# Attention of a four-layer kernel: products for the maxima sent one by one, the second set's maxima turned a stage earlier, the output matrix split in pieces

## The chip, the cores and the metric

The kernel runs on one core of a Trainium2 chip. The metric is the device time of one execution in microseconds; the median of three runs counts. The engines are TensorE (PE; its weight loads are listed as PEld), VectorE (DVE), ScalarE (ACT), GpSimd (POOL), and SyncE (SP), which here only issues DMAs. TensorE's clock is granted at one of two levels, 1.2 and 2.4 GHz; the profile lists it as a share (0.50 or 1.00).

## The reference

Four layers, each followed by a residual addition and a layer norm: a state-space scan, a routed mixture of experts, an attention, and a quantised gated MLP. All is float32. The change touches the attention, of 4 batches x 512 tokens and 32 heads of 16 numbers:

```python
def _L1_attn_ref(x, w_q, w_k, w_v, w_o):
    HEADS = 32
    D_K = HIDDEN // HEADS
    B, S, _ = x.shape

    def proj(w):
        y = jnp.einsum('bsd,ed->bse', x, w)
        return y.reshape(B, S, HEADS, D_K).transpose(0, 2, 1, 3)
    q, k, v = (proj(w_q), proj(w_k), proj(w_v))
    scores = jnp.einsum('bhqd,bhkd->bhqk', q, k) / jnp.sqrt(jnp.float32(D_K))
    attn = jax.nn.softmax(scores, axis=-1)
    out = jnp.einsum('bhqk,bhkd->bhqd', attn, v)
    out = out.transpose(0, 2, 1, 3).reshape(B, S, HIDDEN)
    return jnp.einsum('bse,oe->bso', out, w_o)
...
    x = _layernorm(x + _L1_attn_ref(x, L1_attn_w_q, L1_attn_w_k, L1_attn_w_v, L1_attn_w_o), axis=-1)
```

## The kernel before

The program is a row of stages, each a block in which every engine runs its own list of instructions; a block ends when all engines have ended. Two of them matter here, and what runs behind them is untouched.

**The projection** (`normalise_and_project`, L1487) turns and splits the normalised tokens (each float32 matrix is sent as a high and a low part, three products in `three`, L125 to L129, for one) and makes q, k and v in 48 units (L1533). Twelve matrix products make a unit, into one of four banks `po`. Units 36 to 39 are v of the last block, 40 to 47 its q and k. ScalarE copies each result (L1754, L1761), VectorE makes the low part (L1857), and SP stores them in DRAM (L1623, L1627, L1629).

**The attention** (`attend`, L1888) works on 32 sets of four heads; one set has four steps (128 queries or keys each), 128 steps in all. It makes each score matrix twice. The *first* products (L2035) have the queries in rows; VectorE takes the maximum of each row (L2150). The maxima of a set are negated and split in two parts (L2159, L2163), turned by TensorE into rows (L2042), copied by ScalarE (L2119), and written by DMA below the queries of the set (L1468), so that the *second* products (L2055), with the keys in rows, come out with the maximum already subtracted. ScalarE takes the exponentials (L2111); *weigh* (L2070) multiplies them with v, which also has a column of ones; the result of a set is copied (L2127), turned (L2079) and divided (L2174, L2179).

The first products run eight steps (`LEAD`) ahead of the second. The first eight steps' worth, 16 pairs, is done in the projection (`first`, L1703; `maxima`, L1860), one pair behind each of the units 28 to 43. The maxima of set 0 are turned there too, behind unit 38, into a bank of the first products (L1717), and their rows are copied behind unit 39 (L1776).

A first product has 48 rows of operands, so two of them fit into the two halves of the array; in `attend` they are sent in pairs `first(step, 0)` and `first(step, 1)`, heads 0 and 1, then 2 and 3. They go to three banks in turn (`FIRSTS`, `first_place`); both of a pair wait for their banks before the first is sent (L2029 to L2036). The output's turn takes a place in the same ring of banks. The second products use two pairs of banks; the turn of the maxima takes a place in their ring. The order on TensorE is written out (L2085 to L2099):

```python
for step in range(TOTAL):
    if step + LEAD < TOTAL:
        first(step + LEAD, 0)
    if step:
        weigh(step - 1)
    if kt == 1 and s + 1 < SETS:
        turn_max(s + 1)
    if step + LEAD < TOTAL:
        first(step + LEAD, 1)
    if step + 1 < TOTAL:
        second(step + 1, 0)
        second(step + 1, 1)
    if kt == 2 and s:
        turn_out(s - 1)
```

SP's queue at the start of the attention (L1988): v of set 0, the 12 loads and v of set 3, v of sets 1 and 2, the selecting rows, the 1 MB output matrix (L2369), then for each s the rows of the maxima of set s + 1 and the loads of set s + 4. GpSimd splits the output matrix into two parts, each in one instruction over 2048 columns (`split_wo`, L2372), and later the first weights of the MLP.

## Time and profile before

| | us |
|---|---|
| median of three runs (1920.84 to 1927.97) | 1923.91 |
| the profiled execution | 1923.31 |
| its span, first to last instruction | 1921.6 |
| projection's units with first products, from | 851.5 |
| attention, first instruction to the last turn of an output | 921.98 to 1326 |
| busy over the span: PE, DVE, ACT, POOL | 1718.2, 1475.6, 829.8, 680.0 |
| mean granted TensorE clock | 0.961 |

The profile is of one execution. Its times are microseconds from the span's start unless marked ns. Matrix products are pipelined and their ends are modelled, so their starts are what counts; the timeline merges instructions of one kind that follow one another into one row with a count. A row's last bracket is the time for which the engine sat idle before it and what ended that; "issue" is time in which it waited for nothing that the profile shows.

### The profile page before, as it was taken

The numbers are of one execution on the slowest core, as the hardware profiler recorded it, in microseconds if no ns is written. First come the engines' busy times: TensorE is split into PE (matmuls) and PEld (weight loads), VectorE is DVE, ScalarE is ACT, GpSimd is POOL, SyncE is SP. The second block draws the span as 40 slices with busy tenths as digits, with TensorE's granted clock in tenths as the row PEclk, the third lists the DMA queues.
The fourth block names the chain that finished last, engine by engine and source line by source line (L and its number), as shares of the span: only waits on it lengthen the run. The fifth ranks groups of instructions, "written<-read, shape, count | busy, mean of one in ns | idle before, by whom it ended". The sixth has DMA issues, their size and how long they took to land. (4 is left out here: it accounts for less than half of the span.)

```text
span 1921.6 us, 24417 instructions
## 1 busy us (share of the span) xinstructions
PE 1718.2 (89%) x7762; PEld 1045.0 (54%) x7762; DVE 1475.6 (77%) x2715; ACT 829.8 (43%) x1415; POOL 680.0 (35%) x413
## 2 busy tenths in 40 slices
PE   8999979786959995999788888888989999999997
PEld 2333323224747873876333333334768778778786
DVE  7999999999726666753588888884976776776678
ACT  6657464444203554321477777776521111111112
POOL 5898999994234654300130000000031330330100
PEclk8999999999979997999799999999989999999999
DMA  5434344321147996864543333320010000000002
GB/s 159 122 124 119 117 129 123 91 71 39 67 185 281 414 414 244 278 213 159 138 119 91 91 93 94 94 72 4 1 67 1 33 34 1 34 33 1 1 1 88
DMA packets 111583, 213.27 MB, mean 111 GB/s; under 512 B 19012, under 2 KB 35780, under 8 KB 110554
## 3 DMA queue, kind: packets, MB, share of 16 engines
q1 hardware_dynamic: 106337, 194.94, 31.3%
q0 software_dynamic: 5120, 16.78, 2.6%
q8 instruction: 64, 1.05, 0.2%
q14 instruction: 62, 0.50, 0.1%
HBM read 146.85 MB, written 62.72 MB: 109 GB/s over the span
## 5 line engine op out<-in xcount | busy, mean ns | idle before, releaser
L2150 DVE TENSOR_REDUCE early_top<-att_first 128x1 f32<-128x512 f32 x480 | 311.4, 686 | 52.5 <-PE att_first L2035 45.0
L562 DVE TENSOR_TENSOR_SCAN ssm_h<-ssm_da,ssm_dbx 128x512 f32<-128x512 f32 x256 | 303.8, 1206 | 1.8 <-ACT ssm_da L441 1.5
L283 POOL TENSOR_TENSOR ssm_dbx<-ssm_u,ssm_bbc 128x2048 f32<-128x2048 f32 x63 | 285.6, 4534 | 26.2 <-DVE ssm_h L562 25.7
L2111 ACT ACTIVATE att_prob<-att_second 128x1024 f32<-128x1024 f32 x256 | 248.1, 1022 | 82.8 <-PE att_second L2055 77.7
L653 PE MATMUL ssm_y<-ssm_hc,all_ident 128*128 128x512 f32 x384 | 216.1, 646 | 42.4 <-DVE ssm_hc L528 42.4
L441 ACT ACTIVATE ssm_da<-ssm_dt,ssm_minus_a 128x512 f32<-128x512 f32 x256 | 176.6, 690 | 168.2 <-DVE ssm_h L562 168.1
L2533 ACT ACTIVATE ffn_silu<-ffn_pg 128x256 f32<-128x256 f32 x112 | 43.2, 386 | 407.1 <-PE ffn_pg L129 407.1
L2398 POOL TENSOR_TENSOR pairs_raw<-pairs_raw,pairs_scales 128x512 f32<-128x512 f32 x42 | 42.2, 1043 | 485.3 <-DMA pairs_raw<-in_w 485.3
L127 PE MATMUL ffn_pg<-pairs_wh,last_XH 128*128 128x512 f32 x448 | 176.9, 395 | 1.7 <-PEq L2201 1.7
L128 PE MATMUL ffn_pg<-pairs_wl,last_XH 128*128 128x512 f32 x448 | 176.8, 395 | 0.0
L129 PE MATMUL ffn_pg<-pairs_wh,last_XL 128*128 128x512 f32 x448 | 175.6, 392 | 0.0
L2566 DVE TENSOR_TENSOR ffn_h<-ffn_pg,ffn_silu 128x256 f32<-128x256 f32 x112 | 47.3, 423 | 130.2 <-ACT ffn_silu L2533 130.1
L653 PEld LDWEIGHTS ssm_y<-ssm_hc,all_ident 128*128 128x128 f32 x384 | 65.1, 197 | 140.2 <-DVE ssm_hc L528 93.3
L2070 PE MATMUL att_out<-att_prob,att_v 128*32 128x512 f32 x1024 | 139.8, 619 | 0.2
L528 DVE TENSOR_TENSOR ssm_hc<-ssm_cbc,ssm_h 128x512 f32<-128x512 f32 x192 | 127.5, 664 | 6.2 <-DVE ssm_h L562 4.8
L2405 POOL TENSOR_SCALAR pairs_wh<-pairs_raw 128x512 fp32r<-128x512 f32 x42 | 24.9, 629 | 234.4 <-PE ffn_py L129 234.4
L127 PE MATMUL ffn_py<-pairs_wh,ffn_hh 128*128 128x512 f32 x224 | 98.4, 439 | 0.0
L127 PEld LDWEIGHTS ffn_pg<-pairs_wh,last_XH 128*128 128x128 f32 x448 | 84.8, 189 | 21.9 <-issue 2.1
L2035 PE MATMUL att_first<-early_ks,early_qs 48*128 48x512 f32 x288 | 72.9, 496 | 25.3 <-DVE early_top L2150 23.1
L129 PEld LDWEIGHTS ffn_pg<-pairs_wh,last_XL 128*128 128x128 f32 x448 | 84.8, 189 | 18.8
L128 PEld LDWEIGHTS ffn_pg<-pairs_wl,last_XH 128*128 128x128 f32 x448 | 84.8, 189 | 18.2
L128 PE MATMUL ffn_py<-pairs_wl,ffn_hh 128*128 128x512 f32 x224 | 89.2, 398 | 0.0
(355 smaller groups left out, 3635.0 us busy)
## 6 DMA issues: line engine op xcount, KB each, us to landing
all_X<-in_w SPq DMA_DIRECT2D x29, 769.0 KB, 10.3
ssm_bbc<-brow_dram SPq DMA_DIRECT2D x64, 256.0 KB, 4.2
ssm_cbs<-crow_dram SPq DMA_DIRECT2D x64, 256.0 KB, 3.4
sorted_x<-ssm_zero SPq DMA_DIRECT2D x47, 256.0 KB, 3.6
sorted_y<-exp_y SPq DMA_DIRECT2D x47, 256.0 KB, 10.6
mlps_raw<-in_w SPq DMA_DIRECT2D x14, 769.0 KB, 9.5
pairs_raw<-in_w SPq DMA_DIRECT2D x7, 1536.0 KB, 6.5
v_dram<-all_sums SPq DMA_DIRECT2D x16, 512.0 KB
```

The source lines that it names most:

```text
L127: pe.matmul(out, lh, rh, start=first, stop=False)
L128: pe.matmul(out, lh, rl, start=False, stop=False)
L129: return pe.matmul(out, ll, rh, start=False, stop=last)
L283: nc.gpsimd.tensor_tensor(dbx[:, n % 2], u[:, n // STATE % 2], bbc[:, n % RING, :].unsqueeze(1).to_broadcast([P, KC, NB]), ALU.mult).then_ ...
L441: nc.scalar.activation(da[:, i % 2, :], dt[:, b % 2, c, :], ACT.Exp, scale=minus_a[:, c, n % STATE:n % STATE + 1]).then_inc(da_ready, 1)
L528: nc.vector.tensor_tensor(hc[:, k % 2, :], cbc[:], h[:, n % 2, c, :], ALU.mult).then_inc(hc_ready, 1)
L562: nc.vector.tensor_tensor_scan(h[:, n % 2, c, :], da[:, i % 2, :], dbx[:, n % 2, c, :], 0.0, ALU.mult, ALU.add).then_inc(h_ready, 1)
L653: pe.matmul(y[:, c, :], g.ident[:], hc[:, k % 2, :], start=(m == 0), stop=(m == STATE - 1)).then_inc(y_own, 1)
L2035: pe.matmul(p_first[first_place(m) % FIRSTS][:], qs[w % RING][at, pair, qt * P:(qt + 1) * P], ks[w % RING][at, pair, :], start=True, stop= ...
L2070: mm = pe.matmul(p_out[VPAD * j:VPAD * (j + 1), :], v[s % RING][:, kt, VPAD * j:VPAD * (j + 1)], prob[step % 2][:, j, :], start=(kt == 0), ...
L2111: nc.scalar.activation(prob[step % 2][:, js, :], p_second[second_place(step, pair) % 2][:], ACT.Exp, scale=DK ** -0.5).then_inc(exp_done, 1)
L2150: nc.vector.tensor_reduce(top[w % 2][:, qt, item:item + 1], p_first[first_place(m) % FIRSTS][:], AX.X, ALU.max).then_inc(max_done, 1)
```

## The change

What it does, in `attend`: a first product is sent alone, with a wait for its own bank only, in the order first 0, weigh, turn of the maxima, first 1, first 2, second 0, first 3, second 1, turn of the output. The maxima of set 1 are no longer turned in the attention; they are negated, turned, copied and sent by DMA in the projection, as those of set 0 are. There, negation comes behind unit 36 (44 for set 1), the turn behind unit 37 (45), into the banks of the turned x tiles instead of a bank of the first products, the copy behind unit 38 (46), and the DMA ahead of unit 39's (47's) store. The rows of set 1 have a place of their own, from partition 32 on. The waits for the stores and loads that stood at the end of the projection on SP move into the attention: SP waits for the stores ahead of its first load, TensorE for the loads and rows of a set ahead of its first use, ScalarE and VectorE for the stores ahead of reusing their memory. Two v places and both `o_sb` places use the memory of the projection's `lo` and `hi`. The output matrix is split in four pieces of 512 columns for each part.

```diff
@@ FirstSets
-        self.rows = sb("rows", [2 * SET, NB], F32R)
+        self.minus = [sb(f"minus{k}", [P, QTILES, 2, SET], F32R) for k in range(2)]
+        rows = sb("rows", [32 + 2 * SET, NB], F32R)
+        self.rows = [rows[32 * k:32 * k + 2 * SET, :] for k in range(2)]
@@ normalise_and_project
-        FIRST_UNIT, TURN_UNIT = 28, 38
+        FIRST_UNIT = 28
+        MINUS_UNIT = [FIRST_UNIT + QTILES * PAIRS * (w + 1) for w in range(2)]
+        ROWS_UNIT = [u + 2 for u in MINUS_UNIT]
...
+                if kind == "unit" and k in MINUS_UNIT:
+                    out.append(("minus", MINUS_UNIT.index(k)))
+                if kind == "unit" and k - 1 in MINUS_UNIT:
+                    out.append(("turn", MINUS_UNIT.index(k - 1)))
                 if kind == "unit" and FIRST_UNIT <= k < FIRST_UNIT + f.STEPS * PAIRS:
                     out.append(("first", k - FIRST_UNIT))
-                if (kind, k) == ("unit", TURN_UNIT):
-                    out.append(("turn", 0))
...
+            def send_maxima(w):
+                sp.wait_ge(rows_ready, w + 1)
+                load_row_maxima(sp, f.qs[w], f.rows[w], f.rows_in[w])
...
-                if u == TURN_UNIT + 2:
-                    sp.wait_ge(rows_ready, 1)
-                    load_row_maxima(sp, f.qs[0], f.rows, f.rows_in)
+                if u - 1 in ROWS_UNIT:
+                    send_maxima(ROWS_UNIT.index(u - 1))
...
-            for k in range(2):
-                sp.wait_ge(stored[k], 16 * qk_before(len(units)))
-                sp.wait_ge(v_stored[k], 16 * TILES // 2)
-            for loaded in f.loaded:
-                sp.wait_ge(loaded, 192)
-            sp.wait_ge(f.selected, 32 * f.LOADED)
-            sp.wait_ge(f.rows_in, 32)
...
-                if p == TURN_UNIT - FIRST_UNIT + 1:
-                    pe.wait_ge(rows_ready, 1)
...
-            def turn_max(_):
-                pe.wait_ge(minus_lo, 1)
-                pe.wait_ge(max_done, 2 * (TURN_UNIT - FIRST_UNIT + 1))
+            def turn_max(w):
+                pe.wait_ge(minus_lo, w + 1)
+                pe.wait_ge(xl_ready, TILES)
                 for qt in range(QTILES):
-                    mm = pe.transpose(p_first[0][0:2 * SET, qt * P:(qt + 1) * P],
-                                      minus[:, qt].rearrange("p k h -> p (k h)").bitcast(F32), g.ident[:])
+                    mm = pe.transpose(pt[w][0:2 * SET, qt, :], minus[w][:, qt].rearrange("p k h -> p (k h)").bitcast(F32),
+                                      g.ident[:])
@@ attend
+        EARLY_SETS = 2
...
         @block.sync
         def _(sp):
+            for k in range(2):
+                sp.wait_ge(f.v_stored[k], 16 * TILES // 2)
+                sp.wait_ge(f.stored[k], 32 * UNITS)
             load_v(sp, 0)
             load(sp, f.LOADED)
...
-                if s + 1 < SETS:
+                if EARLY_SETS <= s + 1 < SETS:
                     load_max(sp, s + 1)
...
-            def first(step, pair):
+            def first(step, item):
 
-                w, qt = step // STEPS, step % STEPS
-                if step % STEPS == 0 and pair == 0 and loads(w):
-                    pe.wait_ge(loaded[w % RING], 192 * loads(w))
-                for k in range(2):
-                    m = 4 * step + 2 * pair + k
-                    first_free(first_place(m))
-                for k in range(2):
-                    m = 4 * step + 2 * pair + k
-                    at = slice(k * ROWS, k * ROWS + TERMS)
-                    pe.matmul(p_first[first_place(m) % FIRSTS][:], qs[w % RING][at, pair, qt * P:(qt + 1) * P],
-                              ks[w % RING][at, pair, :], start=True, stop=True).then_inc(first_ready, 1)
+                w, qt, pair, k = step // STEPS, step % STEPS, item // 2, item % 2
+                if step % STEPS == 0 and item == 0:
+                    if loads(w):
+                        pe.wait_ge(loaded[w % RING], 192 * loads(w))
+                    else:
+                        pe.wait_ge(f.loaded[w], 192)
+                m = 4 * step + item
+                first_free(first_place(m))
+                at = slice(k * ROWS, k * ROWS + TERMS)
+                pe.matmul(p_first[first_place(m) % FIRSTS][:], qs[w % RING][at, pair, qt * P:(qt + 1) * P],
+                          ks[w % RING][at, pair, :], start=True, stop=True).then_inc(first_ready, 1)
...
-                if step + LEAD < TOTAL:
+                ahead, more = step + LEAD < TOTAL, step + 1 < TOTAL
+                if ahead:
                     first(step + LEAD, 0)
                 if step:
                     weigh(step - 1)
-                if kt == 1 and s + 1 < SETS:
+                if kt == 1 and EARLY_SETS <= s + 1 < SETS:
                     turn_max(s + 1)
-                if step + LEAD < TOTAL:
+                if ahead:
                     first(step + LEAD, 1)
-                if step + 1 < TOTAL:
+                    first(step + LEAD, 2)
+                if more:
                     second(step + 1, 0)
+                if ahead:
+                    first(step + LEAD, 3)
+                if more:
                     second(step + 1, 1)
@@ PairWeights.split_wo
-        pool.tensor_scalar(self.wo_hi, self.wo_raw, 1.0, 0.0, ALU.mult, ALU.add).then_inc(self.wo_hi_ready, 1)
-        pool.wait_ge(self.wo_hi_ready, 1)
-        pool.tensor_tensor(self.wo_lo, self.wo_raw, self.wo_hi.bitcast(F32), ALU.subtract).then_inc(self.wo_lo_ready, 1)
+        for c in range(KC):
+            at = slice(c * DIM, (c + 1) * DIM)
+            pool.tensor_scalar(self.wo_hi[:, at], self.wo_raw[:, at], 1.0, 0.0, ALU.mult, ALU.add).then_inc(self.wo_hi_ready, 1)
+        for c in range(KC):
+            at = slice(c * DIM, (c + 1) * DIM)
+            pool.wait_ge(self.wo_hi_ready, c + 1)
+            pool.tensor_tensor(self.wo_lo[:, at], self.wo_raw[:, at], self.wo_hi[:, at].bitcast(F32),
+                               ALU.subtract).then_inc(self.wo_lo_ready, 1)
```

## Rows read from the trace of the kernel before

**Rows 1.** the page, costliest groups, the row of VectorE's maxima (section 5)

```profile
L2150 DVE TENSOR_REDUCE early_top<-att_first 128x1 f32<-128x512 f32 x480 | 311.4, 686 | 52.5 <-PE att_first L2035 45.0
```

**Rows 2.** timeline, steady steps: start us, us, engine, line, op; idle before, releaser

```profile
1099.41 2.62 DVE L2150 TENSOR_REDUCE early_top<-att_first 128x1 f32<-128x512 f32 x4
...
1108.39 0.50 PE L2035 MATMUL att_first<-early_ks,early_qs 48*128 48x512 f32 x2
...
1108.92 2.10 DVE L2150 TENSOR_REDUCE early_top<-att_first 128x1 f32<-128x512 f32 x3 [0.17 <-PE att_first L2035]
...
1109.76 0.49 PE L2035 MATMUL att_first<-early_ks,early_qs 48*128 48x512 f32 x2 [0.40 <-DVE early_top L2150]
...
1110.19 1.06 PE L2070 MATMUL att_out<-att_prob,att_v 128*32 128x512 f32 x8
...
1111.18 0.49 PE L2035 MATMUL att_first<-early_ks,early_qs 48*128 48x512 f32 x2
```

**Rows 3.** the same timeline: one set, the turn of the maxima

```profile
1100.25 0.49 PE L2035 MATMUL att_first<-early_ks,early_qs 48*128 48x512 f32 x2 [0.40 <-DVE early_top L2150]
...
1101.67 0.60 PE L2042 MATMUL att_second<-all_ident,att_minus 128*8 128x128 f32 x4
...
1102.20 0.50 PE L2035 MATMUL att_first<-early_ks,early_qs 48*128 48x512 f32 x2
...
1112.55 0.49 PE L2035 MATMUL att_first<-early_ks,early_qs 48*128 48x512 f32 x2 [0.40 <-DVE early_top L2150]
```

**Rows 4.** timeline of the projection around the turn of set 0

```profile
882.27 0.50 PE L1714 MATMUL proj_first<-early_ks,early_qs 48*128 48x512 f32 x2
...
885.68 0.50 PE L1714 MATMUL proj_first<-early_ks,early_qs 48*128 48x512 f32 x2
...
887.85 0.60 PE L1721 MATMUL proj_first<-all_ident,proj_minus 128*8 128x128 f32 x4 [1.67 <-DVE proj_minus L1872]
...
892.46 0.49 PE L1714 MATMUL proj_first<-early_ks,early_qs 48*128 48x512 f32 x2 [1.25 <-ACT early_rows L1776]
```

**Rows 5.** timeline of the boundary between projection and attention

```profile
917.63 0.40 PE L129 MATMUL proj_po<-later_XH,proj_wl 128*128 128x512 f32 x1
...
921.95 0.38 SPq L1969 DMA_DIRECT2D att_v<-v_dram  x1
...
921.98 1.22 PE L2055 MATMUL att_second<-early_qs,early_ks 56*128 56x512 f32 x4 [3.96 <-PEq L1489]
...
926.77 1.93 PE L2070 MATMUL att_out<-att_prob,att_v 128*32 128x512 f32 x8
```

**Rows 6.** SP queue's waits, 900:1000: total us, times, longest us

```profile
SPq L1635 <- DMA qk_dram<-proj_lo: 1.5, 1, 1.5
```

**Rows 7.** timeline of the attention's first two sets, 928 to 961 us

```profile
928.63 1.02 PE L2042 MATMUL att_second<-all_ident,att_minus 128*8 128x128 f32 x4
...
935.47 0.51 PE L2035 MATMUL att_first<-early_ks,early_qs 48*128 48x512 f32 x2
...
940.08 1.22 PE L2055 MATMUL att_second<-early_qs,early_ks 56*128 56x512 f32 x4 [4.10 <-DMA early_qs<-att_rows]
...
942.62 4.52 POOL L2376 TENSOR_TENSOR pairs_wl<-pairs_raw,pairs_wh 128x2048 fp32r<-128x2048 f32 x1
943.11 4.07 DVE L2163 SCALAR_TENSOR_TENSOR att_minus<-early_top,att_minus 128x16 fp32r<-128x16 f32 x1
...
947.92 0.80 PE L2035 MATMUL att_first<-att_ks,att_qs 48*128 48x512 f32 x2 [3.21 <-DVE early_top L2150]
...
960.96 0.51 PE L2035 MATMUL att_first<-att_ks,att_qs 48*128 48x512 f32 x2 [0.40 <-DVE early_top L2150]
```

**Rows 8.** 4 us stretches: PE, PEld, DVE, ACT, POOL busy, PEclk, DMA, GB/s

```profile
922.00:926.00 4.00, 3.25 (x12) 1.63 (x12) 2.24 (x6) 3.50 (x4) 0.00 (x0) 0.50 0.52 152
950.00:954.00 4.00, 3.98 (x20) 1.61 (x20) 1.38 (x4) 1.84 (x3) 0.00 (x0) 0.50 0.06 8
962.00:966.00 4.00, 3.59 (x30) 1.41 (x24) 3.50 (x8) 3.03 (x5) 0.00 (x0) 1.00 0.94 166
```

More of the change, by code:

```diff
@@ L1878, in _ @@
             for kind, k in with_firsts(order):
-                {"tile": tile, "unit": unit, "first": maxima, "turn": minus_max}[kind](k)
+                if kind != "turn":
+                    {"tile": tile, "unit": unit, "first": maxima, "minus": minus_max}[kind](k)
                 if (kind, k) == ("tile", 0):
@@ L1933, in maxima_before @@
         def maxima_before(step):
-            return len([t for t in range(step) if t % STEPS == 1 and t // STEPS + 1 < SETS])
+            return len([t for t in range(step) if t % STEPS == 1 and EARLY_SETS <= t // STEPS + 1 < SETS])
         def first_place(m):
@@ L1955, in attend @@
         second_at = {second_place(step, pair): 2 * step + pair for step in range(TOTAL) for pair in range(2)}
-        maxima_at = {maxima_place(w): w for w in range(1, SETS)}
+        maxima_at = {maxima_place(w): w for w in range(EARLY_SETS, SETS)}
         def loads(w):
@@ L2172, in divide @@
                     dve.wait_ge(o_done, s)
+                else:
+                    for k in range(2):
+                        dve.wait_ge(f.v_stored[k], 16 * TILES // 2)
                 o = p_first[out_place(s) % FIRSTS][:].rearrange("p (t h d) -> p t h d", t=STEPS, h=SET)
```

95 lines of the change are left out of this document (55 added, 40 removed).

## The prediction

> **What bounds the kernel now.** I read the page's groups first, then the stretch of the attention engine by engine, then its timeline step by step. The largest VectorE group is the maximum of the first product, 480 reductions of 686 ns, with 52.5 us of idle time before them, most of it put down to the first products [rows 1]. So VectorE looks like the bound with a little air, and the change aims at that air. The timeline says more exactly what the air is [rows 2]. A regular step repeats every 2.79 us (the pair of first products behind the weighing goes out at 1108.39 and at 1111.18). Four reductions back to back take 2.62 us (1099.41, x4). The step is therefore not set by VectorE alone but by a loop through both engines: that pair goes out at 1108.39, its reduction starts at 1108.92 (+0.53), when that is over the next pair goes out at 1109.76 (+0.84), the weighing with the probabilities follows at 1110.19 (+0.43), and behind it the next half-step pair at 1111.18 (+0.99). The sum is 2.79 us, 0.17 more than VectorE needs. A step with the turn of the maxima has 0.53 us more in the loop (transposes at 1101.67, product at 1102.20), one with the turn of the output and the division is longer by 0.6, and a set of four steps takes 12.30 us (1100.25 to 1112.55) [rows 3]. The other sets from about 1000 us on run at this pace.
>
> The beginning of the attention does not. From its first instruction, at 921.98, to the first product of its ninth step, at 960.96, it takes 39 us, where two sets want 24.6. The timeline of that stretch shows why [rows 5, 7].
>
> **Part 1: the turn in the projection.** TensorE bounds this stretch: from one lone pair of first products to the next takes 3.41 us (882.27 to 885.68). Around the turn of set 0 it takes 6.78 us (885.68 to 892.46): first TensorE waits 1.67 us for the maxima just negated, turns them at 887.85, and later the next pair waits 1.25 us until ScalarE has read the bank that the turn used [rows 4]. Extra: 6.78 - 3.41 = 3.37 us. Afterwards the maxima are negated one unit ahead of the turn, the turn goes to a bank of the x tiles, which is free, and the wait for the copied rows is gone. What stays is four small transposes; in the attention they cost TensorE 0.53 us [rows 3], and two waits of 1.67 and 1.25 us taken from 3.37 leave 0.45. There are now two turns, 1.06 us at the higher price. Net 3.37 - 1.06 = **2.3 us gained** (up to 2.5). The second copy (0.57 us on ScalarE) and its two DMAs on SP's queue lie ahead of the last unit's store, in a stretch where SP waits for that unit anyway; cover gone, they would cost about that much, 0.57 us and the issue of two DMAs.
>
> **Part 2: the end of the projection.** The last product starts at 917.63 and the attention's first at 921.98 [rows 5]. SP held the block open for the last stores to land, 1.5 us [rows 6]. These waits move behind the boundary, ahead of SP's first v load. Behind them stand the loads of v, of set 3, and the output matrix. The v load goes out when its stores have landed, as now, but without the boundary behind that, so not later than 921.95; the first weighing was at 926.77 [rows 5] and comes to 925.3. Between issue and use lay 4.8 us and lie at least 3.3; a load that needed all 4.8 would give the 1.5 back. **1.5 us gained** (ends 0 and 1.5). The added waits of TensorE, ScalarE and VectorE are for loads and stores landed by then.
>
> **Part 3: the attention no longer turns set 1.** In step 1 the transposes took 1.02 us of TensorE at the low clock (928.63) [rows 7]: **1.0 us gained**. Much more hangs on the transfer of the rows. Issued right behind the output matrix, it let TensorE wait 4.10 us for it before the product at 940.08 [rows 7]. Afterwards these rows travel during the projection: **4.1 us gained**. What is late next? The loads of sets 3 and 4, needed at steps 4 and 8. The first are issued before the matrix, and the pair of first products that read them behind 940.08 waited for nothing of theirs; the second have one load less ahead of them than now.
>
> **Part 4: the output matrix in pieces.** GpSimd's subtraction over 2048 columns runs 4.52 us from 942.62, and in it the small VectorE operation on the maxima, over 16 numbers a partition, takes 4.07 us; the pair of first products at 947.92 waits 3.21 us for VectorE [rows 7], where a regular one waits 0.40 [rows 2]. That is 2.8 us. A piece of a quarter holds VectorE a quarter as long, an estimate of 1.1 us from the 4.52; GpSimd's sum may grow a little, off the path. Besides, without the losses of part 3 the operation comes at about 936, before the matrix has landed (GpSimd begins to subtract at 942.62, 1.9 us after it); the next is 12.3 us later, at about 948, where GpSimd is just through, give or take 1 us. **2.8 us gained**, less 0.5 for one such meeting.
>
> **Part 5: the clock.** The granted clock is 1.00 in 962:966, the 2.4 GHz level. It is 0.50 (1.2 GHz) in 922:926, after TensorE's gap at the boundary, and again in 950:954, after the wait for the rows and the hold [rows 8]. Without losses step 4 would have begun at 935.47 + 1.37 = 936.84 (its half-step in the steady part, 1109.76 less 1108.39 [rows 2]). From there to step 8 at 960.96 [rows 7] there are 24.1 us; one set of 12.3 is wanted; 11.8 are lost; 4.1 and 2.8 are named above, and the remaining **4.9 us** are steps at the lower clock. With both stalls gone TensorE does there what it does in the steady part, where the clock never fell, so I take the 4.9 us in full (ends: 0 and 4.9). Whether the gap at the boundary, now 4.0 - 1.5 = 2.5 us instead of 4.0, still brings the clock down I cannot tell: the waits of 1.67 and 1.25 us around the projection's turn brought none down. I leave the first low stretch as it was; without it there would be up to 1.5 us more (from 921.98 to 936.84 are 14.9 us, against 12.3 for a set, less the 1.0 counted).
>
> **Part 6: the products sent alone.** The loop of [rows 2] has to be redone for the order first 0, weighing, first 1, first 2, second, first 3, second. With three banks, product i needs the reduction of i-3. Product 0 of the next step needs product 1 of this one reduced; product 1 is sent behind the weighing. So: product 1 to its reduction 0.53, reduction and signal 0.84, product 0 to weighing 0.43, weighing to product 1 0.99. It is the same 2.79 us; product 1 has merely taken the place of product 2. VectorE's 0.17 us of idle time move with it. The reason is that in either order three reductions (1.97 us) cover the time from one reading to the next reduction behind the weighing. In a step with the output's turn, the turn waits for product 1's reduction, takes the 0.6 us that it takes now, and the next product 0 is let go by VectorE at that same time, 1.9 to 2.0 us after product 1. So **0 us**, with ends of -0.02 and +0.05 us in each of 120 steps: -2 and +6 us. What hides the extra work on TensorE: product 3 alone takes up to another 0.22 us (an estimate: half of the 0.43 from product to weighing, which holds one product's columns and the change of layout), against 0.4 us of idle time before each step's first pair [rows 2].
> The trace shows two products of a pair going through side by side: half the rows of the array each. The Trainium skill, TensorEngine Tiling (Array Packing), section "Key Properties", states this in general: different tiles can load and multiply in parallel. Read against this change, products sent alone give that up; read closely, products 1 and 2, and product 3 and the next second, still lie in different halves. By the first reading TensorE has 0.44 us more in a step and the slower rival below holds, by the second the sum above.
>
> **The sum.** 2.3 + 1.5 + 1.0 + 4.1 + 2.3 + 4.9 + 0 = 16.1 us. The profiled execution took 1923.31 us (span 1921.6), 0.6 below the median of 1923.91: 1907.2 by the one, 1907.8 by the other, **1907.5 us**. A measurement can tell about 0.5% (10 us) from no change here; the three times shown span 0.4%.
>
> **The rivals.**
> 1. *The new order frees VectorE.* If sending a product alone shortens the way to the weighing or lets products run ahead, each regular step falls to VectorE's 2.62 us: 0.17 x 120 = 20 us more, 1887 us. For it: 52.5 us of idle before the reductions [rows 1]. Against: the loop above. Chance 0.13.
> 2. *The second low stretch stays, or something else is late at the start* (the v load, a DMA behind the matrix, another hold by GpSimd). Then 5 to 10 of the 16 us are missing: 1912 to 1918 us. Chance 0.17.
> 3. *Slower: TensorE becomes the bound of the step.* Product 3 waits for its bank between the two second products, keeps the second of them back, and the next product 0 comes late. Where: from product 1 to the next product 0. Price: what this takes beyond 1.37 us, in 120 steps. I have it at 1.0 to 1.2 us; the lone halves at worst add 0.44, that is 1.6, 0.25 late: 30 us, 1937 us. From 0.14 us a step on it eats the start's gain. For it: the second products, the transposes and product 0 all stand behind that wait. Against: 0.4 us idle now, and the bank is free 0.55 us after product 1. Chance 0.08.
> 4. *It does little:* the start's losses are mostly of this execution, or they return in another place. 1918 to 1924 us. Chance 0.05.
>
> **How the numbers follow.** My forecast, 1902 to 1912 us, has 0.57. Rivals 1 to 4 have 0.13, 0.17, 0.08 and 0.05. The range of 1896 to 1917 us holds the forecast with its ends, nearly all of rival 2 and a part of rival 1 (a half-used gain); outside remain the full rival 1, rival 3 and half of 4. Faster by over 0.5% (below 1914.3): 0.57 + 0.13 + 0.14 = 0.84; within 0.5%: 0.03 + 0.05 + 0.01 = 0.09; slower: 0.07.
>
> **What would show it.** Regular steps of 2.79 us with the idle time now before product 1's reduction, 12.3 us a set; two spacings of lone pairs near 3.9 us in the projection, and none of 6.8; 2.5 us from the last product to the attention's first; no wait of the second products on the rows' DMA; no operation on the maxima of 4 us; the ninth step's first product 25 to 27 us after the attention's first instruction instead of 39. The forecast fails if the steps are shorter than 2.75 us (rival 1) or longer than 2.85 (rival 3), or if the granted clock between 930 and 960 is still at 0.5 for more than 3 us.

## The result, and the profile after

The changed kernel takes 1902.8 us (median of 4 runs, 1899.69 to 1903.57) against 1924.93 us for the kernel before (median of 4 runs, one more than in the table of before). The ratio is 0.9885, with a 95% interval of 0.9869 to 0.9901. That is 22 us less by the medians and 19.8 us less by the spans of the two profiled executions (1921.6 and 1901.8 us). The forecast was 1907.5 us.

The page of the changed kernel, groups of instructions (busy time, mean ns, idle time before them and what ended it). The first line answers the one of [rows 1]: 3.9 us less idle time in front of the reductions, and 3 ns less for each.

```profile
L2178 DVE TENSOR_REDUCE early_top<-att_first 128x1 f32<-128x512 f32 x480 | 302.9, 683 | 48.6 <-PE att_first L2049 48.6
...
L2049 PE MATMUL att_first<-early_ks,early_qs 48*128 48x512 f32 x288 | 102.3, 483 | 6.8 <-DVE early_top L2178 5.1
```

The timeline of a steady stretch of the changed kernel, which answers [rows 2] (start, duration, engine, line, operation, count; in brackets the idle time before it and its releaser):

```profile
1107.42 0.50 PE L2049 MATMUL att_first<-early_ks,early_qs 48*128 48x512 f32 x2
...
1107.96 2.48 DVE L2178 TENSOR_REDUCE early_top<-att_first 128x1 f32<-128x512 f32 x4 [0.25 <-PE att_first L2049]
...
1108.76 0.18 PEld L2049 LDWEIGHTS att_first<-early_ks,early_qs 48*128 48x128 f32 x1 [0.57 <-issue]
1108.80 0.47 PE L2049 MATMUL att_first<-early_ks,early_qs 48*128 48x512 f32 x1 [0.15 <-DVE early_top L2178]
1109.19 0.43 SPq L1980 DMA_DIRECT2D early_lo<-v_dram  x1
1109.19 0.16 PEld L2090 LDWEIGHTS att_out<-att_prob,early_lo 128*32 128x32 f32 x8 [0.24 <-issue]
...
1110.19 0.50 PE L2049 MATMUL att_first<-early_ks,early_qs 48*128 48x512 f32 x2
...
1111.47 0.18 PEld L2049 LDWEIGHTS att_first<-early_ks,early_qs 48*128 48x128 f32 x1 [0.51 <-DVE early_top L2178]
1111.47 0.50 PE L2049 MATMUL att_first<-early_ks,early_qs 48*128 48x512 f32 x1
1111.90 0.16 PEld L2090 LDWEIGHTS att_out<-att_prob,att_v 128*32 128x32 f32 x8 [0.25 <-issue]
```

From product 1 to the next step's product 0 it takes 1.38 us where that next step opens a set (1107.42 to 1108.80), and 1.28 us (1110.19 to 1111.47) in two of the other three; before, it took 1.37 us in all three of these [rows 2]. In the fourth, with the output's turn, it takes 1.93 us and took 1.97 before. The product at 1108.80 stands behind two waits, for a reduction and for the set's loads, and its weight load is 0.04 us ahead of it. The one at 1111.47 stands behind a single wait, and weight load and product start together. The four reductions at 1107.96 take 2.48 us, that is (2.48 - 0.68) / 3 = 0.60 us from one to the next. I had read 2.62 us for four in [rows 2] as VectorE's own pace; it isn't. The 0.60 us stand in the trace of before as well: it is the shortest spacing there too.

VectorE's first operation on a set's maxima comes once in each set, and so marks the sets. On the left of each line is its start, then its duration. The first sets of the changed kernel's attention, from its timeline of VectorE's line, and beneath them GpSimd's work from its own timeline:

```profile
937.63 0.16 DVE L2186 TENSOR_SCALAR early_minus<-early_top 128x16 fp32r<-128x16 f32 x1
949.86 0.17 DVE L2186 TENSOR_SCALAR early_minus<-early_top 128x16 fp32r<-128x16 f32 x1
961.92 0.84 DVE L2186 TENSOR_SCALAR early_minus<-early_top 128x16 fp32r<-128x16 f32 x1
974.36 2.32 DVE L2186 TENSOR_SCALAR early_minus<-early_top 128x16 fp32r<-128x16 f32 x1
989.84 0.16 DVE L2186 TENSOR_SCALAR early_minus<-early_top 128x16 fp32r<-128x16 f32 x1
```

```profile
940.20 4.98 POOL L2410 TENSOR_TENSOR pairs_wl<-pairs_raw,pairs_wh 128x512 fp32r<-128x512 f32 x4
959.69 6.04 POOL L2433 TENSOR_TENSOR pairs_raw<-pairs_raw,pairs_scales 128x512 f32<-128x512 f32 x6 [14.51 <-DMA pairs_raw<-in_w]
965.69 3.54 POOL L2440 TENSOR_SCALAR pairs_wh<-pairs_raw 128x512 fp32r<-128x512 f32 x6
969.19 7.46 POOL L2444 TENSOR_TENSOR pairs_wl<-pairs_raw,pairs_wh 128x512 fp32r<-128x512 f32 x6
```

The sets take 12.23, 12.06, 12.44 and 15.48 us, and 12.05 us from there on. In the 15.48 us GpSimd kept the small operation back for 2.32 us, and TensorE's clock fell once more:

```profile
977.00:981.00 4.00, 3.67 (x15) 0.98 (x17) 2.15 (x5) 0.05 (x1) 0.00 (x0) 0.57 0.00 0
```

7.46 us for six pieces are 1.24 us from one to the next, so the operation falls into the fifth piece (about 974.1 to 975.4) and ends, at 976.68, with the sixth. The Trainium skill, SBUF — State Buffer, section "SBUF: two separate sides", says that an operation of GpSimd, or of VectorE under certain conditions, holds their shared port as an exclusive lock for the whole instruction. The blocking agrees, the limit of one instruction does not always. At 961.92 and at 963.27 VectorE's operations on maxima ended 0.03 us after the one piece (L2433, 1.0 us apart) that they met first. Under the subtraction of the pair of weights (L2444), in all nine profiles in which an operation arrived ahead of the last piece, it was held until the last one had ended. What makes the difference stays open. Such a case, GpSimd at work when VectorE comes to its small operation on the maxima, is called a meeting below.

The end of the projection and the attention's beginning, in the timeline (it answers [rows 4] and [rows 5]). A lone pair is a pair of first products between two units of the projection.

```profile
880.10 0.51 PE L1717 MATMUL proj_first<-early_ks,early_qs 48*128 48x512 f32 x2
...
883.43 0.60 PE L1724 MATMUL proj_pt<-all_ident,early_minus 128*8 128x128 f32 x4
...
883.96 0.50 PE L1717 MATMUL proj_first<-early_ks,early_qs 48*128 48x512 f32 x2
...
916.11 0.40 PE L129 MATMUL proj_po<-later_XH,proj_wl 128*128 128x512 f32 x1
...
918.81 0.79 PE L2075 MATMUL att_second<-early_qs,early_ks 56*128 56x512 f32 x4 [2.31 <-PEq L1493]
...
924.22 1.08 PE L2090 MATMUL att_out<-att_prob,att_v 128*32 128x512 f32 x4 [1.10 <-DMA att_v<-v_dram]
...
948.30 0.47 PE L2049 MATMUL att_first<-att_ks,att_qs 48*128 48x512 f32 x1 [0.17 <-DVE early_top L2178]
```

And the same beginning in stretches of 4 us (columns as in [rows 8]; the granted clock is the number behind the engines' columns). It stood at 0.50, the 1.2 GHz level, for nearly all of the time from 919 to 936 us, and at 1.00 from then to 963; the low level of 950 to 954 in [rows 8] is gone.

```profile
915.00:919.00 4.00, 1.70 (x9) 1.13 (x9) 0.80 (x2) 0.98 (x2) 0.00 (x0) 1.00 0.67 225
919.00:923.00 4.00, 3.40 (x13) 1.64 (x11) 2.58 (x4) 3.99 (x5) 0.00 (x0) 0.54 0.48 150
923.00:927.00 4.00, 2.90 (x13) 1.02 (x14) 0.78 (x2) 0.79 (x1) 0.00 (x0) 0.50 0.54 152
927.00:931.00 4.00, 4.00 (x18) 1.49 (x18) 2.40 (x4) 1.94 (x2) 0.00 (x0) 0.50 0.91 250
931.00:935.00 4.00, 4.00 (x20) 1.48 (x16) 2.48 (x4) 1.94 (x2) 0.00 (x0) 0.50 1.02 290
935.00:939.00 4.00, 3.91 (x24) 1.86 (x20) 3.40 (x7) 3.10 (x4) 1.15 (x2) 0.82 1.10 191
```

Where the 19.8 us of the profiled executions went:

| stretch | before | after | difference |
|---|---|---|---|
| projection, second lone pair to last product | 62.64 | 59.86 | -2.8 |
| boundary, product to product | 4.35 | 2.70 | -1.65 |
| attention's first product to its ninth step | 38.98 | 29.49 | -9.5 |
| the 27 sets behind that, to the first product 0 of the last one | 333.5 | 329.2 | -4.35 |
| end of the attention, and what follows it | | | -2.8 |
| everything ahead of the projection's second lone pair | | | +1.3 |

### The profile page after: what moved, and what is told of

The parts are those of the page before. It is cut to its first block and busy times, and to the rows that moved or that the text cites. A ratio compares the mean times of both kernels' runs of the same rounds, so it can differ in the third digit from the quotient of the medians.

```text
span 1901.8 us, 24215 instructions
## 1 busy us (share of the span) xinstructions
PE 1733.0 (91%) x7762; PEld 1063.8 (56%) x7762; DVE 1465.6 (77%) x2715; ACT 829.6 (44%) x1415; POOL 679.4 (36%) x419
## 5 line engine op out<-in xcount | busy, mean ns | idle before, releaser
L2178 DVE TENSOR_REDUCE early_top<-att_first 128x1 f32<-128x512 f32 x480 | 302.9, 683 | 48.6 <-PE att_first L2049 48.6
L2433 POOL TENSOR_TENSOR pairs_raw<-pairs_raw,pairs_scales 128x512 f32<-128x512 f32 x42 | 42.3, 1044 | 466.8 <-DMA pairs_raw<-in_w 466.8
L2049 PE MATMUL att_first<-early_ks,early_qs 48*128 48x512 f32 x288 | 102.3, 483 | 6.8 <-DVE early_top L2178 5.1
L2049 PEld LDWEIGHTS att_first<-early_ks,early_qs 48*128 48x128 f32 x288 | 41.4, 190 | 85.3 <-DVE early_top L2178 55.3
L2090 PE MATMUL att_out<-att_prob,att_v 128*32 128x512 f32 x640 | 87.8, 622 | 1.3 <-DMA att_v<-v_dram 1.1
```

The lines of the kernel that those rows point to most:

```text
L2049: pe.matmul(p_first[first_place(m) % FIRSTS][:], qs[w % RING][at, pair, qt * P:(qt + 1) * P], ks[w % RING][at, pair, :], start=True, stop= ...
L2090: mm = pe.matmul(p_out[VPAD * j:VPAD * (j + 1), :], v[s % RING][:, kt, VPAD * j:VPAD * (j + 1)], prob[step % 2][:, j, :], start=(kt == 0), ...
L2178: nc.vector.tensor_reduce(top[w % 2][:, qt, item:item + 1], p_first[first_place(m) % FIRSTS][:], AX.X, ALU.max).then_inc(max_done, 1)
```

## The experiments

Three questions were open: why the regular sets became 0.26 us shorter, which no step of the forecast had; what the start's 9.5 us consist of; and whether the pieces of the output matrix do anything. The kernels ran on three chips, so each is compared by its ratio to the kernel before on the same chip, and by stretches of its profile.

### What shortens a set: the order, or the number of waits?

The changed kernel with a second wait ahead of each lone product (on the bank before it, which the reductions have passed anyway):

```diff
+                if first_place(m) - FIRSTS - 1 in first_at:
+                    first_free(first_place(m) - 1)
                 first_free(first_place(m))
```

> The changed kernel with one more wait ahead of each first product, on a bank that is already free (the one sent before it), so each product has two waits as each pair of the kernel before had. Theory of the waits: the 0.09 us a step by which the changed kernel's sets are shorter (12.05 us against 12.30) come from products that have one wait, which then rides on the weight load; with two, the late one rides on the product and costs 0.09 us more. Then the sets go back to 12.25 to 12.35 us and the time is 6 to 8 us longer than that of the changed kernel (about 1909). Theory of the order: sending alone and the new order made it; then the sets stay at 12.05 and the time at about 1902.5.

Measured: ratio 0.9914 (0.9884 to 0.9945), sets of 12.19 us; the 0.03 us between weight load and product 0 are there again in every step. That is half of the way back, short of the 12.25 to 12.35 expected. From product 1 to product 0 it takes 1.37 us again, but from product 0, where it has two waits, to product 1 only 1.39 us instead of 1.42: 0.03 us of each 0.09 come back.

The order of before in the changed kernel, pairs again, with one wait ahead of each pair (on the bank that comes free later):

```diff
@@ in first()
-                first_free(first_place(m))
+                if item % 2 == 0:
+                    first_free(first_place(m + 1))
@@ the order
                     first(step + LEAD, 0)
+                    first(step + LEAD, 1)
...
                 if ahead:
-                    first(step + LEAD, 1)
                     first(step + LEAD, 2)
+                    first(step + LEAD, 3)
                 if more:
                     second(step + 1, 0)
-                if ahead:
-                    first(step + LEAD, 3)
-                if more:
                     second(step + 1, 1)
```

> The changed kernel with the order of before (0 and 1, weighing, turn, 2 and 3, both seconds), but with a single wait for each pair, on the bank that comes free last. Theory of the waits: the loop is the same in either order, so the sets stay at 12.05 us (up to 0.05 either way) and the time at about 1902.5. Theory of the order: the sets are back at 12.30 and the time is 6 to 8 us longer.

Measured: 0.9888 (0.9862 to 0.9914), sets of 12.05 us. And the same with both waits of before ahead of the pair:

```diff
                 if item % 2 == 0:
+                    first_free(first_place(m))
                     first_free(first_place(m + 1))
```

> Only this part of the change undone: order and waits of before, all else as changed. Both theories: sets of 12.30 us, 6 to 8 us longer than the changed kernel, about 1909. It is the control for the two others. If it stays below 12.15, the shorter set came from another part of the change.

Measured: 0.9923 (0.9894 to 0.9951), sets of 12.32 us. These two kernels ran on one chip and differ in that wait alone: 1879.33 us (at most 1880.75) against 1885.64 us (at least 1882.88), 6.3 us by the medians. So with one wait both orders take 12.05 us, and with two waits the old order takes what the kernel before takes (12.32 us, its median). The step in which even the changed kernel has two waits is the one that opens a set; there the load's wait was moved up to the product before:

```diff
-                if step % STEPS == 0 and item == 0:
-                    if loads(w):
-                        pe.wait_ge(loaded[w % RING], 192 * loads(w))
...
+                if step % STEPS == STEPS - 1 and item == 3 and step + 1 < TOTAL:
+                    if loads(w + 1):
+                        pe.wait_ge(loaded[(w + 1) % RING], 192 * loads(w + 1))
...
```

> The changed kernel with the wait for a set's loads moved from its first product to the last product of the step before, which has time to spare. Theory of the waits: product 0 of each set's first step has one wait instead of two and goes 0.09 us earlier, so the sets take 11.94 to 11.98 us and the time falls by 2 to 3 us. Theory of the order: no change.

Measured: 0.9875 (0.9836 to 0.9914), sets of 11.99 us, so 0.06 us less and not 0.09: product 0 goes 0.09 us earlier, and product 1 follows it 0.03 us later. A gain of this size can't be told from none by the total time. Last, the test from the other side: the kernel before, untouched but for one wait in place of two where both banks of a pair are freed by reductions.

```diff
-                for k in range(2):
-                    m = 4 * step + 2 * pair + k
-                    first_free(first_place(m))
+                m = 4 * step + 2 * pair
+                if not (first_place(m) - FIRSTS in first_at and first_place(m + 1) - FIRSTS in first_at):
+                    first_free(first_place(m))
+                first_free(first_place(m + 1))
```

> The kernel before, whole, with one wait in place of two ahead of each pair of first products in the attention. Theory (the second wait ahead of a product was the cost, the order of the products is worth nothing): the gap from the end of a reduction to the next first product falls by about 0.09 us, a regular set takes 12.05 instead of 12.32 us, 27 sets give 7 us, and the kernel takes about 0.996 of the time before. Rival (the order of products is what shortens the steps, and the waits cost only in company of the new order): sets stay at 12.3 and the time is the time before within 2 us.

Measured: 1915.03 us against 1926.51, 0.9944 (0.9928 to 0.9961). Its timeline, two sets' marks and one half-step:

```profile
1104.73 0.17 DVE L2160 TENSOR_SCALAR att_minus<-early_top 128x16 fp32r<-128x16 f32 x1
...
1108.21 0.50 PE L2036 MATMUL att_first<-early_ks,early_qs 48*128 48x512 f32 x2
...
1109.49 0.19 PEld L2036 LDWEIGHTS att_first<-early_ks,early_qs 48*128 48x128 f32 x2 [0.35 <-DVE early_top L2151]
1109.49 0.49 PE L2036 MATMUL att_first<-early_ks,early_qs 48*128 48x512 f32 x2
...
1116.75 0.16 DVE L2160 TENSOR_SCALAR att_minus<-early_top 128x16 fp32r<-128x16 f32 x1
```

A set is 12.02 here (12.05 as the median of all), and pair to pair is 1.28 us instead of 1.37. The gain was 0.56% where I expected 0.4%; against the profile of the kernel before there are 2.9 us at the start, 7.9 us in the 28 sets behind it, and 1.1 us after the attention. Only the 7.9 us are surely the wait's: at the start the clock also stood low for 3.4 us less, and nothing was changed behind the attention. In the changed kernel it is 0.26 us in each of 27 sets, 7.1 of the 19.8 us, so about a third of what the change brings comes from one wait less ahead of a product. The order of the products, the change's largest edit, is worth nothing with one wait; with two, sending alone is worth 0.13 us a set (12.19 against 12.32).

The Trainium skill, Perfetto Trace Analysis, section "Identifying Dependency Chains", states that an instruction that waits on several engines can have extra semaphore instructions put in front. The traces show such instructions here, though both waits are for VectorE. These are the ones of the line that waits for a reduction, in the kernel before and in this one (count, ns, first and last start):

```profile
L2014 PEldq EVENT_SEMAPHORE  x270: 51/51/51, 925.9 to 1324.0; - x135
L2014 PEldq EVENT_SEMAPHORE  x90: 51/51/51, 939.6 to 1313.5; - x90
```

The 180 that are gone, six a set in 30 sets, are all by which the two profiles differ (24417 and 24237 instructions). Three of the six stand ahead of a product 0 that waits for a reduction.

### What the start consists of

Control on the second chip, the changed kernel once more:

> The changed kernel itself, for the comparison with the three others on this chip. From the attention's first product to the ninth step's first product 29.5 us (the first chip's record), sets of 12.05 us, and a low granted clock of TensorE for 14 to 17 us from the boundary on.

Measured: 0.9884 (0.9864 to 0.9904), sets of 12.05 us, and one of 14.97 where GpSimd's pieces are met. Then part 3 undone: set 1's maxima are turned in the attention again, all else as changed.

```diff
-        MINUS_UNIT = [FIRST_UNIT + QTILES * PAIRS * (w + 1) for w in range(2)]
+        MINUS_UNIT = [FIRST_UNIT + QTILES * PAIRS * (w + 1) for w in range(1)]
...
-            if ROWS_UNIT[1] + 1 >= len(units):
-                send_maxima(1)
...
-        EARLY_SETS = 2
+        EARLY_SETS = 1
...
```

> The changed kernel with the maxima of set 1 turned, copied and sent in the attention again (part 3 undone), all else as changed. The forecast's account: TensorE waits some 4 us for these rows behind the output matrix, the turn costs 1.0 us, and the wait brings the clock down a second time (up to 4.9 us); the projection is 0.45 us shorter. Then it is 8 to 10 us slower than the changed kernel. Rival: only the wait and the turn count, the clock is low there in any case; then 4.5 to 5.5 us.

Measured: 0.9902 (0.9883 to 0.992), 4.1 us above the control by the medians, 6.8 us by the spans of the profiles: less than the 8 to 10 expected, and near the rival's 4.5 to 5.5. The timeline of its start shows the price, and the windows the clock behind the wait:

```profile
902.38 0.40 SPq L2398 DMA_DIRECT2D pairs_raw<-in_woT  x1
...
902.83 1.47 SPq L1468 DMA_DIRECT2D early_qs<-early_rows  x2
...
913.03 1.22 PE L2073 MATMUL att_second<-early_qs,early_ks 56*128 56x512 f32 x3 [7.63 <-DMA early_qs<-early_rows]
```

```profile
900.00:906.00 6.00, 5.22 (x34) 1.76 (x30) 5.54 (x9) 4.02 (x5) 0.00 (x0) 1.00 0.87 242
906.00:917.00 11.00, 3.97 (x18) 1.52 (x20) 2.64 (x5) 2.33 (x3) 4.43 (x6) 0.53 0.57 154
```

The rows' transfer, issued right behind the output matrix, is awaited for 7.6 us, where the kernel before waited 4.1 [rows 7]; the start takes 7.0 us more than in the control. The mechanism of part 3 holds. So does that of part 5: the wait brings a second low stretch (0.53 in 906 to 917 us), as in the kernel before. It did not cost the full price in this execution, because the first stretch lasted 6.8 us and not 13.7; together they are 3.4 us longer than the control's one.

SP's waits at the attention's start: the load of v behind the wait for v's stores alone, and the wait for the stores of the query and key rows behind it:

```diff
             for k in range(2):
                 sp.wait_ge(f.v_stored[k], 16 * TILES // 2)
-                sp.wait_ge(f.stored[k], 32 * UNITS)
             load_v(sp, 0)
+            for k in range(2):
+                sp.wait_ge(f.stored[k], 32 * UNITS)
             load(sp, f.LOADED)
```

> The changed kernel with the first v load behind the wait for the stored v alone, ahead of the wait for the stored q and k. The first weighing waited 1.10 us for that load, which SP issued 1.6 us after it could have. Theory: the wait goes and the ninth step comes 1.1 to 2 us earlier. Rival: the loads of q and k then crowd it, or the low clock hides it: under 0.5 us.

Measured: 0.9882 (0.9861 to 0.9904), within 1 us of the control. The weighing no longer waits for v, and the start was 2.0 us shorter in this profile. Eight products that nobody reads, at the end of the projection, to keep TensorE busy over the boundary:

```diff
+            pe.wait_ge(rows_ready, 1)
+            for _ in range(8):
+                pe.matmul(pt[0][:].rearrange("p c k -> p (c k)"), g.XH[:, 0, 0:P], g.XH[:, 0, 0:NB], start=True, stop=True)
```

> The changed kernel with eight products that nobody reads at the end of the projection, about 1.8 us, while TensorE would wait for the block's end. Theory of the gap: TensorE's 2.3 us without work at the boundary brings the clock down; filled, it stays at 1.00, steps 1 to 3 take 2.8 us instead of 4.15, and 4 to 5 us are gained. Rival: the attention's opening (few products, the wait for v) brings it down by itself; then the low stretch stays and the time is the same within 1 us.

Measured: 0.9894 (0.9876 to 0.9913). TensorE's wait at the boundary fell from 2.3 to 0.5 us, but the clock fell all the same, 3.4 us behind the attention's first product instead of with it, and stood at its lower level for 13.7 us, as in the control. The time is 2.1 us above the control's. The theory of the gap fails; what brings the clock down is then the attention's opening or something that neither kernel isolates.

Put side by side, the starts follow one number, the time that the clock stands low. From the attention's first product to the start of its 33rd reduction, that is of the ninth step's first, in all profiles without the wait for rows:

| low clock, us | start, us |
|---|---|
| 6.8 | 27.1 (late_split), 27.1 (best), 27.2 (v_load_first) |
| 10.2 | 28.4 (matrix_in_one_piece) |
| 13.7 | 29.1, 29.2, 29.4, 29.9 (pairs_one_wait, changed_again, second_wait, filler) |
| 17.1 | 30.2, 30.3, 30.5 (loads_waited_earlier, pairs_two_waits, the changed kernel) |

That is (30.3 - 27.1) / (17.1 - 6.8) = 0.31 us for each microsecond at the lower level, an estimate from differences between executions; the table shows that the two go together. late_split's start is the changed kernel's, instruction for instruction, still with 0.9 us of waiting for v, and took 27.1 us. So the 2.0 us of v_load_first can't be put down to the v load; they may be the clock alone. What sets the length of the low stretch in one execution stays open.

### What the pieces are worth, and where GpSimd hurts

Part 4 undone, the output matrix split by one operation for each half:

```diff
-        for c in range(KC):
...
+        pool.tensor_scalar(self.wo_hi, self.wo_raw, 1.0, 0.0, ALU.mult, ALU.add).then_inc(self.wo_hi_ready, 1)
+        pool.wait_ge(self.wo_hi_ready, 1)
+        pool.tensor_tensor(self.wo_lo, self.wo_raw, self.wo_hi.bitcast(F32), ALU.subtract).then_inc(self.wo_lo_ready, 1)
...
```

> The changed kernel with the output matrix split again by one long operation for each half. Theory: at the place where the pieces now stand no operation of VectorE on the maxima meets them for more than a few tenths of a microsecond (in the changed kernel the one that met them took 0.31 us), so the whole form costs at most what one blocked operation lasts. If minus_high or minus_low of a set meets the long operation it is held for up to 4 us and the time is 2 to 4 us above the changed kernel; if it does not, the time is the same within 1 us. Rival (forecast): the pieces are worth 2.3 us wherever the maxima stand.

Measured: 1901.62 us, 0.9871 (0.9851 to 0.989). Nothing is lost that the total time could show. In its timeline the long subtraction runs between two operations on the maxima and meets neither:

```profile
935.55 0.16 DVE L2190 SCALAR_TENSOR_TENSOR early_minus<-early_top,early_minus 128x16 fp32r<-128x16 f32 x1
...
940.65 4.57 POOL L2406 TENSOR_TENSOR pairs_wl<-pairs_raw,pairs_wh 128x2048 fp32r<-128x2048 f32 x1
...
946.63 0.17 DVE L2186 TENSOR_SCALAR early_minus<-early_top 128x16 fp32r<-128x16 f32 x1
```

The meetings are with the pair of weights here too: the first four sets take 12.05, 13.96, 13.34 and 12.23 us, 3.4 us more than regular ones, where the changed kernel's first four take 4.0 us more.

GpSimd's preparation of the first pair of weights, whose pieces the changed kernel met at 974, held back until the last sets:

```diff
             g.pair_weights.split_wo(pool)
+            pool.wait_ge(pv_done, STEPS * (SETS - 2) + 2)
             g.pair_weights.first_split(pool)
```

> The changed kernel with GpSimd's preparation of the first pair of weights held back until the last sets of the attention, where no operation of VectorE on maxima is left to meet it. Theory: the two long sets (12.44 and 15.47 us in the changed kernel's profile) become regular ones of 12.05, and the time falls by 3 to 4 us, ratio about 0.9865 against the kernel before. Rival: the long set has its own cause (a fall of TensorE's clock without GpSimd), or the weights come late after the attention, and the time stays or rises by up to 3 us.

Measured: 1903.64 us, 0.9887 (0.987 to 0.9905); no gain. The sets behave as the theory says: every one takes 12.02 to 12.07 us up to the last, and the stretch behind the ninth step is 4.0 us shorter than in the changed kernel. But I had put the wait too late. Timeline of its end:

```profile
1292.99 7.40 POOL L2445 TENSOR_TENSOR pairs_wl<-pairs_raw,pairs_wh 128x512 fp32r<-128x512 f32 x6
...
1297.49 0.42 DVE L2210 TENSOR_TENSOR all_sums<-att_first,att_rec 128x256 f32<-128x256 f32 x1
1300.71 1.57 PEld L2268 LDWEIGHTS out_pt<-all_ident,all_sums 128*128 128x128 f32 x8 [3.79 <-issue]
```

GpSimd ends at 1300.39, 2.5 us after VectorE's last operation, and the block ends with its slowest engine; TensorE stands still, and then runs at the lower level. All that follows the attention took 6.3 us more than in the changed kernel's profile.

The last kernel has the earlier load wait, the v load first and the late split together:

> The changed kernel with three things together: the wait for the loads of a set one item earlier, the load of v ahead of the wait for the rows at the start of the attention, and GpSimd's preparation held back. If they add: 27 x 0.06 = 1.5 us, 1 to 2 us at the start and 3 to 4 us at the meetings, in all 6 us below the changed kernel, a ratio of about 0.985 against the kernel before. Rival: the gains of the start are taken back by TensorE's low clock, and together they give 3 us, ratio 0.987.

Measured: 1901.22 us, 0.9875 (0.9855 to 0.9894). Its attention is the shortest of all (27.1 us for the start, sets of 11.99), and it gives 5.1 us of that back at the same place as late_split. No kernel of these beats the changed one by more than the intervals.

## Why the prediction was right, and where it was wrong

The time lies in the range, 4.7 us below the forecast, and the sum of 16.1 us stands against 19.8 in the profiles. That is partly luck: the start gave 2.8 us less than forecast and the later meetings took 2.8 us, while the sets gave 7.1 us that no term had and the part behind the attention 2.8. Parts 1 and 2 are read from the profiles of before and after; no run undoes them by themselves.

**Part 1, the turn in the projection: right.** The first turn costs 0.45 us (880.10 to 883.96 is 3.86 us, against 3.41 [rows 4]). The second lies behind the last lone pair, so there is one spacing near 3.9 us and not the two forecast; from that pair to the projection's last product it takes 11.74 us instead of 11.50, so this turn costs 0.24. The stretch became 2.8 us shorter, 2.3 were forecast. No spacing of 6.8 is left.

**Part 2, the boundary: right.** 2.70 us from product to product where it was 4.35, so -1.65 us, and 2.31 us of idle time where 2.5 were forecast. The v load did not move up with the boundary: it went out 4.2 us behind the projection's last product (920.32 less 916.11), against 4.3 before [rows 5]. So the weighing came 5.4 us after the attention's first product instead of 4.8, and waited 1.1 us for v; the experiments show no cost of that wait.

**Part 3, no turn of set 1: right**, and the cost shown by undoing it, 4 to 7 us against 5.1 forecast. The loads of sets 3 and 4 were in time.

**Part 4, the pieces: wrong.** The hold of 4.07 us [rows 7] is gone, but because the maxima come earlier, which the forecast named second, and not because of the pieces; with the matrix in one piece it is gone too. Nor was it close: GpSimd's subtraction ended at 945.18, 4.7 us ahead of the next operation on the maxima, where the forecast had "just through, give or take 1 us". What failed is looking at the matrix alone: behind it GpSimd prepares the pair of weights, whose operations moved against the sets just as well. There the meetings cost 1.05 us before and 3.8 us after. Nor is a piece the upper bound of a hold: the estimate of 1.1 us for one meeting stands against 2.32 us, two pieces long.

**Part 5, the clock: half right.** The low stretches behind the first are gone, as forecast, and undoing part 3 brings one back. Their size was about right: 17.0 us at 0.31 us each are 5.3 us, an estimate, against the 4.9 forecast. The first did not stay "as it was": it lasted 17.1 us in the changed kernel's profile, against 10.2 before (where two more, of 6.8 and 10.2 us, came behind it); at 0.31 us each these 7 us are 2.1 us, again an estimate, most of the 2.8 us by which the start missed its 12.3. The ninth step's first product came after 29.5 us and not 25 to 27. By my own sign (clock at 0.5 for more than 3 us after 930) this was a miss, though in late_split's profile, with the same code up to there, it came after 26.2 us.

**Part 6, the order: right by itself, and wrong in the sum.** The new order is worth 0, as worked out, once each product or pair has one wait. But the loop's second term, "reduction and signal 0.84", was taken as a constant of the hardware, when 0.09 us of it came from the second of two waits ahead of the pair. The change drops that wait because a lone product needs one bank only, and the term becomes 0.75. With three such steps in a set, that is 0.27 us a set with pairs and 0.26 in the new order, in 27 sets 7.1 us. I listed what the change adds in waits but never counted what it removes from the ones in front of the products. The regular steps, at 1.28 + 1.42 = 2.70 us, are below the bound of 2.75 that I had named as the sign of failure.

**The rivals.** Rival 1 (VectorE set free, steps of 2.62 us) had the direction right, by another mechanism and for a third of its price; its premise, that VectorE needs 2.62 us for four reductions, is refuted by the 2.48 us above. VectorE had some 0.4 us of idle time in each step, not 0.17. Rival 2 (something else is late at the start) happened in part: the longer low stretch, the meeting at 974. Rival 3 (TensorE becomes the bound) is refuted: product 1 to product 0 fell to 1.28 us, and the pairs of before take the same with one wait.

**What no step had:** 2.5 us after the attention, 1.6 of them where TensorE's clock was low in the kernel before (1329.7 to 1333.2 us) and not in the changed one; and 1.3 us the other way ahead of the projection's second lone pair. As that low stretch comes and goes among the kernels here, I take it for a difference of executions, which was not tested by itself.

## What to carry to other kernels

Count the waits in front of the instruction that closes a loop between two engines. If semaphores are counted in order, the later wait contains the earlier, and dropping the earlier one gave 0.56% here, half of what the whole change gave (1.15%), by an edit of four lines; the rewritten order gave nothing beside it.

An interval between two operations in a trace is the engine's own pace only if nothing released them; look for the shortest spacing of the same operation anywhere in the kernel before calling an engine nearly full.

When a start becomes shorter, look at what else runs beside the sets behind it on an engine with a timetable of its own: cutting one operation of GpSimd in pieces did nothing, while the next job, already in pieces, took 3 us back, with the matrix in pieces or whole. Holding such a job until the end only moves its cost to the block's end if it is not over by then.

## What the runs showed of the hardware that was not expected

- A second wait ahead of a TensorE product, satisfied 0.7 us or more before, cost 0.09 us where the product waited for the other one: from the end of a reduction to the next product 0.054 to 0.058 us with one wait and 0.146 to 0.150 with two (medians by place in the set). With one wait the weight load is held together with its product; with two it starts 0.03 us ahead of it, and an EVENT_SEMAPHORE of 51 ns stands ahead of it in the queue.
- VectorE started reductions of 128x512 numbers every 0.60 us, though each is listed with 0.683 us: the listed times overlap.
- A VectorE operation over 16 numbers a partition, 0.16 us alone, was held for 2.32 us by two GpSimd operations 1.24 us apart (in set1_in_attention for 2.95 us, by three). It did not get its turn between them, while under two other rows of pieces (L2433 here, the output matrix's in set1_in_attention) it did.
- The low stretch of TensorE's clock at the boundary lasted 6.8, 10.2, 13.7 or 17.1 us in executions whose instructions up to there were the same or nearly so, and came even with TensorE's wait cut to 0.5 us by products for nothing.
